# Sixteen 4x8 pixel groups per partition in place of eight 8x8 ones, with the Newton steps on VectorE, in a fused four-layer kernel

## The reference

```python
x = x + L0(x, dx, angle)      # every pixel of the image, rotated and shifted, bilinear:
    # out = g(iy0,ix0)*(wy0*wx0) + g(iy0,ix1)*(wy0*wx1) + g(iy1,ix0)*(wy1*wx0) + g(iy1,ix1)*(wy1*wx1)
    # with g(y, x) the pixel, or 0 outside of the image
x = x + L1(x, expert)         # relu(x wi^T + common and expert LoRA) wo^T + common and expert LoRA
x = x + L2(x, kind)           # softmax(mask(tanh(x W1 + b1) v)) x / count
x = x + L3(x, language)       # h = x + relu(x w1 + b1) w2 + b2;
    # (h - mean) * rsqrt(var + 1e-5) * gamma + beta, over the 512 columns
```

## Time and profile before

| | |
|---|---|
| median of 3 runs | 2329.93 us (2317.05 to 2334.8) |
| profiled execution | 2330.62 us, span 2328.9 us, granted TensorE clock 0.948 |
| share of the span | PE 92%, DVE 84%, POOL 41%, ACT 38% |
| chain that ended last | PE 40%, DVE 38%, issue 13%, DVE's sequencer 5% |
| DMA | 303.63 MB, mean 130 GB/s |

### The profile page before, as it was taken

How to read it: one execution, slowest core, us unless ns; L and a number is a source line. 1 busy time by engine, 2 the same in 40 slices (tenths; PEclk the granted TensorE clock), 3 DMA queues, 4 the chain that set the end, 5 groups by cost and what they waited for, 6 DMA issues and landing times.

```text
span 2328.9 us, 53794 instructions
## 1 busy us (share of the span) xinstructions
PE 2142.4 (92%) x15230; PEld 1350.8 (58%) x15230; DVE 1964.8 (84%) x6594; ACT 874.8 (38%) x2292; POOL 948.5 (41%) x1066
## 2 busy tenths in 40 slices
PE   7679999989989999999999899899999999999996
PEld 2345666656555665665556566565665655566663
DVE  7578899889889898889988898898988888899943
ACT  1323444434333443343334334343433333344431
POOL 3424454354354345435342443444445443444201
PEclk6559999999999999999999999999999999999997
DMA  8673555565455556545555655565566445554322
GB/s 223 154 203 94 127 138 138 127 149 126 122 124 134 124 132 151 126 118 128 142 128 118 151 126 135 111 138 133 133 136 147 123 110 132 129 132 116 101 72 63
DMA packets 336494, 303.63 MB, mean 130 GB/s; under 512 B 187295, under 2 KB 255977, under 8 KB 335767
## 3 DMA queue, kind: packets, MB, share of 16 engines
q1 hardware_dynamic: 290358, 184.05, 32.6%
q0 software_dynamic: 42624, 109.35, 20.1%
q10 hardware_dynamic: 3168, 6.29, 0.9%
HBM read 273.73 MB, written 65.70 MB: 146 GB/s over the span
## 4 chain that ended last, share of the span: by engine, by line
PE 40%; DVE 38%; issue 13%; DVEq 5%; SPq 2%; DMA 1%; another core or an unknown queue 0%; ACT 0%; POOL 0%; POOLq 0%; ACTq 0%
DVE work L853 14%; PE bank L1343 13%; PE bank L1380 13%; DVE work L866 3%; DVE work L867 3%; DVE work L865 3%; PE bank L1374 2%; PE bank L1199 2%; DVEq L849 2%; PE bank L1301 2%; DVEq L838 2%; DVE work L809 2%; DVE warp_sum L880 1%; PE bank L1275 1%; DVE hidden_parts L913 1%
## 5 line engine op out<-in xcount | busy, mean ns | idle before, releaser
L1343 PE MATMUL bank<-x1T,wiT 128*128 128x256 f16 x6144 | 764.5, 275 | 18.0 <-issue 17.2
L1380 PE MATMUL bank<-woT,hidden_parts 128*128 128x512 f16 x3072 | 759.8, 384 | 0.0
L853 DVE TENSOR_TENSOR work<-work 128x72 f32<-128x72 f32 x4096 | 683.2, 282 | 72.6 <-issue 50.6
L584 POOL DMA_INDIRECT work<-strips,gather_now x512 | 676.9, 1322 | 158.9 <-issue 136.3
L1343 PEld LDWEIGHTS bank<-x1T,wiT 128*128 128x128 f16 x6144 | 601.5, 99 | 165.9 <-issue 70.9
L1167 ACT ACTIVATE hidden<-bank 128x256 f32<-128x256 f32 x512 | 196.1, 383 | 774.7 <-PE bank L1350 446.3
L1380 PEld LDWEIGHTS bank<-woT,hidden_parts 128*128 128x128 f16 x3072 | 260.2, 98 | 301.8 <-issue 11.4
L580 POOL TENSOR_TENSOR gather_now<-group_now,no_offset 128x8 int32<-128x8 int32 x64 | 30.5, 476 | 801.3 <-DVE work L853 801.3
L913 DVE TENSOR_TENSOR hidden_parts<-hidden,hidden_parts 128x512 f16<-128x512 f32 x256 | 176.7, 690 | 29.4 <-ACT hidden_parts L1169 13.7
L1169 ACT ACTIVATE hidden_parts<-bank 128x256 f16<-128x256 f32 x512 | 195.1, 381 | 0.0
L1374 PE MATMUL bank<-hidden_parts,experts 128*32 128x128 f16 x2048 | 151.0, 226 | 0.0
(11 more groups left out here) (191 smaller groups left out, 2394.0 us busy)
## 6 DMA issues: line engine op xcount, KB each, us to landing
strips<-in_x_dram SPq DMA_DIRECT2D x64, 532.0 KB
lw<-in_L_cond_W_dram SPq DMA_DIRECT2D x128, 256.0 KB, 3.1
xs<-in_x_dram SPq DMA_DIRECT2D x64, 256.0 KB
experts<-ib_dram SPq DMA_DIRECT2D x64, 256.0 KB
gamma_b<-in_L_cond_gamma_dram SPq DMA_DIRECT2D x64, 256.0 KB, 4.4
x<-in_L_cond_beta_dram POOLq DMA_DIRECT2D x64, 256.0 KB, 5.7
out_dram<-y SPq DMA_DIRECT2D x64, 256.0 KB, 2.5
work<-strips,gather_now POOLq DMA_INDIRECT x512
```

The costliest lines, as they stand in the source:

```text
L584: g.indirect_dma_start(out=win[:, k, gi, :], out_offset=None, in_=flat, in_offset=bass.IndirectOffsetOnAxis(at, 0)).then_inc(gathered[k], 16)
L853: last = v.tensor_tensor(prods[:, :, :, j, :, row].rearrange("p a b g -> p g b a"), seen, wx.unsqueeze(2).broadcast_to([128, NG, TAPS, TAP ...
L1343: t.matmul(b[:, 0:2 * T], wiT[:, ws, m, tile(f)], x1T[:, xs_, m, :], start=(m == 0 and ws + xs_ == 0), stop=False)
L1380: last = t.matmul(down_ps[k][:, :], hidden_parts[:, hs, f % RING, k * T:(k + 1) * T], woT[:, ws, f, :], start=(first and n == 0), stop=False)
```

## The change

- A partition's pixels are 16 groups of 4x8 (`GC` columns, `GR` rows). An image has 32 offsets in place of 64, and a product covers 144 values in place of 72. There are 16 windows of 128 x 226 values per image in place of 8 of 128 x 348, each by its own indirect DMA. Strips are 64 wide, three DMAs per image. The tables of groups double.
- The three Newton steps go from POOL to DVE (three small operations each). The guess, the steps and `finish(i-2)` stand behind `add_pooled(1)`.
- DVE's loop takes four pairs per turn, 6 turns in place of 13.
- The setup's temporaries lie in `work`, 1024 wide in place of 512.

```diff
-GP = 8
-NG = 8
-Q = GP * GP
+GC, GR = 4, 8
+NG = 16
+Q = GC * GR
...
-SW, SS = 76, 32
+SW, SS = 64, 32
...
-RUN = 4 * SW + 44
+RUN = 3 * SW + 34
...
-                src = bass.AP(img.tensor, img.offset, [[SS, NS - 5], [D, T], [1, SW]])
-                sp.dma_start(strips[s, 2:NS - 3, rows, :], src).then_inc(strips_in[s], 16)
+                src = bass.AP(img.tensor, img.offset, [[SS, NS - 3], [D, T], [1, SW]])
+                sp.dma_start(strips[s, 1:NS - 2, rows, :], src).then_inc(strips_in[s], 16)
...
-            def deviations(c):
...
             def body(i, q):
                 if there(i, 2):
                     add_beta(i - 2, q)
-                    deviations(i - 2)
...
-                        products(0, 0, 0, 16)
+                        products(0, 0, 0, 8)
...
-                    if there(i, 2):
-                        guess_deviations()
...
                     if tail:
                         mask_scores(0)
-                    if there(i, 2):
-                        finish(i - 2)
                     if tail:
                         mask_scores(1)
...
                 if tail:
                     add_pooled(1)
+                if there(i, 2):
+                    deviations()
+                    finish(i - 2)
                 if warp:
                     products(1, 0, 0, HALF // 2)
...
+                def deviations():
...
+                    for step in range(3):
+                        link(v.tensor_tensor(newton[:, :], rstd[:, :], rstd[:, :], ALU.mult))
+                        link(v.scalar_tensor_tensor(newton[:, :], newton[:, :], -0.5, var_eps[:, :], ALU.mult, ALU.mult))
+                        link(v.scalar_tensor_tensor(rstd[:, :], newton[:, :], 1.5, rstd[:, :], ALU.add, ALU.mult))
...
-            with dve.Fori(2, NP // 2 - 1) as i:
-                body(i * 2 - 1, 1, first=False)
-                body(i * 2, 0)
-                body(i * 2 + 1, 1, second=False)
+            with dve.Fori(1, NP // 4 - 1) as i:
+                body(i * 4 - 1, 1, first=False)
+                for n in range(3):
+                    body(i * 4 + n, n % 2)
+                body(i * 4 + 3, 1, second=False)
```

More of the change, by code:

```diff
@@ L391, in load_strips @@
                 rows = slice(PADY, PADY + T)
-                src = bass.AP(img.tensor, img.offset, [[SS, NS - 5], [D, T], [1, SW]])
-                sp.dma_start(strips[s, 2:NS - 3, rows, :], src).then_inc(strips_in[s], 16)
-                for n in range(2):
-                    before = LEFT - n * SS
-                    sp.dma_start(strips[s, n, rows, before:SW], img[:, 0:SW - before]).then_inc(strips_in[s], 16)
-                    left = LEFT - n * SS
-                    sp.dma_start(strips[s, NS - 3 + n, rows, 0:left], img[:, D - left:D]).then_inc(strips_in[s], 16)
+                src = bass.AP(img.tensor, img.offset, [[SS, NS - 3], [D, T], [1, SW]])
+                sp.dma_start(strips[s, 1:NS - 2, rows, :], src).then_inc(strips_in[s], 16)
+                sp.dma_start(strips[s, 0, rows, LEFT:SW], img[:, 0:SW - LEFT]).then_inc(strips_in[s], 16)
+                sp.dma_start(strips[s, NS - 2, rows, 0:SS], img[:, D - SS:D]).then_inc(strips_in[s], 16)
             def load_pix(a, k, par):
@@ L564, in _ @@
             for k in range(2):
[L565 removed]
+                pool.wait_ge(strips_in[k], 48)
             for t in range(KT):
@@ L720, in floor @@
                 link(v.tensor_tensor(whole, whole, over, ALU.subtract))
-            xs_flat = xs[:, 1, :, :].rearrange("p k d -> p (k d)")
-            x1T_flat = x1T[:, :, :, :].rearrange("p s k t -> p (s k t)").bitcast(fp32)
             M = B * NG
             shape = lambda t: t.rearrange("p (b g) -> p b g", g=NG)
-            pos, other = xs_flat[:, 0:M], xs_flat[:, M:2 * M]
-            whole, whole_i = x1T_flat[:, 0:M], x1T_flat[:, M:2 * M].bitcast(i32)
-            at_f = y[:, 1, 0:M]
+            pos, other, whole, whole_i, at_f = (work[:, (n + 4) * M:(n + 5) * M] for n in range(5))
+            whole_i = whole_i.bitcast(i32)
             for ax in range(2):
@@ L794, in _ @@
             evacuate_low(11)
-            regs = [ctx.enter_context(v.register(f"window_offset{n}")) for n in range(LOADED)]
-            tap = taps.rearrange("p (x t j g i) -> p x t j g i", x=2, t=TAPS, g=NG, i=GP)
+            regs = [ctx.enter_context(v.register(f"window_offset{n}")) for n in range(HALF)]
+            tap = taps.rearrange("p (x t j g i) -> p x t j g i", x=2, t=TAPS, g=NG, i=GR)
             tap_rows = taps.rearrange("p (x t m) -> p x t m", x=2, t=TAPS)
-            prods = prod.rearrange("p (a b j g i) -> p a b j g i", a=TAPS, b=TAPS, g=NG, i=GP)
+            prods = prod.rearrange("p (a b j g i) -> p a b j g i", a=TAPS, b=TAPS, g=NG, i=GR)
             by_column_tap = prod.rearrange("p (a b m) -> p a b m", a=TAPS, b=TAPS)
@@ L845, in products @@
                     for m in range(start, end):
-                        j, row = m // GP, m % GP
+                        j, row = m // GR, m % GR
                         if m == 0:
@@ L981, in body @@
                             load_offsets(0, part)
-                        products(0, 0, 0, 16)
+                        products(0, 0, 0, 8)
                     if warp:
-                        products(0, 0, 16, 24)
+                        products(0, 0, 8, 12)
                     if ffn:
@@ L991, in body @@
                             residual(k)
-                    if there(i, 2):
-                        guess_deviations()
                     if warp:
-                        products(0, 0, 24, HALF)
+                        products(0, 0, 12, HALF)
                     hidden_low(0)
@@ L1008, in body @@
                 if warp:
-                    products(0, 1, 0, 8)
+                    products(0, 1, 0, 4)
                 hidden_low(2)
                 if warp:
-                    products(0, 1, 8, HALF)
+                    products(0, 1, 4, HALF)
                     take_offsets(1)
@@ L1029, in body @@
                 if warp:
-                    products(1, 1, 0, 24)
+                    products(1, 1, 0, 12)
                 hidden_low(6)
                 if warp:
-                    products(1, 1, 24, HALF)
+                    products(1, 1, 12, HALF)
                 if tail:
@@ L1050, in body @@
                 if ahead:
-                    products(0, 0, 0, 16, w + 1)
+                    products(0, 0, 0, 8, w + 1)
                 if ffn:
@@ L1057, in _ @@
             body(3, 1, second=False)
-            with dve.Fori(2, NP // 2 - 1) as i:
-                body(i * 2 - 1, 1, first=False)
-                body(i * 2, 0)
-                body(i * 2 + 1, 1, second=False)
-            body(NP - 3, 1, first=False)
-            for i in range(NP - 2, NP + 2):
+            with dve.Fori(1, NP // 4 - 1) as i:
[3 more added lines that the diff above has]
+                body(i * 4 + 3, 1, second=False)
+            body(NP - 5, 1, first=False)
+            for i in range(NP - 4, NP + 2):
                 body(i, i % 2)
```

71 lines of the change are left out of this document (25 added, 46 removed).

## The result

The changed kernel takes 2934.52 us (median of 4 runs, 2914.08 to 2949.42) against 2323.91 us of the kernel before on the same chip: a ratio of 1.262, interval 1.256 to 1.267. The forecast was 2326, with a range to 2390. It is 609 us off in the time, and none of the four cases in it is what happened. The times in this document are medians of all runs; one of four runs of `paced` (2851 us) was in a slower state of the chip, and its ratio leaves it out.

The account below looks back on a forecast made before the run. PE and DVE run level, DVE slightly ahead as the bound. From 2330.6 us, some 30 pairs give -16.5, setup +15 and the end -3, so 2326 us; range 2250 to 2390.

Parts of the forecast that it names:

- four cases: Forecast of 2326 us (0.46), no adapter wait (0.25), clock brought down (0.23), POOL late with its gathers (0.06).
- Gathers: On POOL, 16 gathers per image take 20 to 30 us in place of 10 to 16; cost nothing, covered by slack.
- The new wait at the adapter product: PE waits for adapter loads queued on SP behind the moved finish: 2.7 us per pair, 2.1 before an allowance for gathers.
- the sign that I named: PE's adapter product waiting 2 to 3 us for the adapter's transfers in nearly all of 29 pairs.
- S: Start of PE's second pooled product; `y` ready at S + 5.7, first adapter at S + 13.2, PE there at S + 11.1.
- Products: On DVE, 144 values at 0.23 us each, bounds 0.22 and 0.314; DVE gains 5.4 us per pair, bounds 6.0 and 0.
- VectorE's turn: Loop turn every fourth pair, not second: two PE waits of 3.97 us at the pooled product go per four pairs (-7.9).
- Newton on VectorE: Nine more small operations cost DVE 1.8 us per pair; guess and finish only moved; DVE's net gain 3.6 us.
- Setup: Larger group tables and 8 more first gathers before the loop: net +15 us, between +8 and +24; first L1391 at 176.
- The sum: Four pairs 268.1 us, 0.55 less per pair, a pair at 67.0; with setup and end, 2326 us.
- C, the clock: Rival: adapter waits near 4 us bring PE's granted clock to 0.95; 2400 us or somewhat under; chance 0.23.
- D, POOL late: Rival: 16 gathers of image 0 take 36 us, so the next pair's first products wait; 2370 and more; chance 0.06.

Follow-up runs that it names:

- paced: The changed kernel with a pause of 24 small memsets on POOL between an image's eighth and ninth gather; 2818 us, ratio 1.206 to the kernel before.
- late_pace1: The changed kernel with one small memset on POOL ahead of each gather but an image's first; 2349 us, ratio 1.004 to the kernel before.
- split_windows: The kernel before with each window fetched in two halves, so 16 gathers per image and the same bytes; 2661 us, ratio 1.140.
- no_groups: The kernel before with everything of the change but the groups, so still 8 gathers per image; 2447 us, ratio 1.050.
- no_groups_early: The kernel before with Newton steps on VectorE and four pairs per turn, but guess, steps and finish at their old places; 2322 us, ratio 0.997.
- loop4_only: The kernel before with only VectorE's loop changed, four pairs per turn in place of two; 2315 us, ratio 0.987.

## Why the prediction was wrong, step by step

**Gathers: "Cost nothing; the slack is the cover".** This is the step that failed: the term that I put at nothing was worth 585 us, the distance from the changed kernel to `late_pace1`. I priced the 512 further gathers as POOL's and the DMA engines' time only. As such they were what I had: undisturbed 0.95 + 0.30 us each, POOL at 41%, DMA half busy, and no wait for gathered windows in the middle of the run. What they cost lies on the engines that don't gather. From about the tenth of a row PE and SP, and in part VectorE, go on in steps of 0.70 us, for some 10 us, twice in most pairs. Two things seem to make it worse than twice the number: 16 follow each other without a break, which `paced` bears out, and VectorE has fewer runs of products left to hold them up (mean of a gather 1047 ns, 1322 before), for which `split_windows` speaks (1356 ns, 82 steps). I had read the gathers of 5.02 us as POOL's loss; by this they kept the rate down. A sign of it stood in the trace before, in "issue" at the transposes and L1343, which I put down to the loop's turn.

The rule of the Trainium skill, page "SBUF — State Buffer", section "Who interferes with whom", on the port that VectorE and GpSimd share, names those two engines alone. Here PE and SP are slowed, also while VectorE is busy for only 3.32 of 16 us (the fourth window above), so what I had weighed by that rule doesn't bear on the loss.

**The new wait at the adapter product.** Right in size, once the gathers are spaced: in `late_pace1` PE waits 64.3 us there in 25 waits that the profile puts down to the transfer, 2.6 each, where 2.7 were forecast (7 more are called "issue", one of them 8.2 us long). In the changed kernel itself the sign that I named is absent: its adapter product L1291 waits for the transfer once, for 0.7 us. In `no_groups` one pair reads so, PE's timeline first, then VectorE's and PE's again:

```profile
1316.54 1.10 PE L1282 MATMUL bank<-x,probsT 128*128 128x512 f32 x2
```

```profile
1322.00 1.41 DVE L942 SCALAR_TENSOR_TENSOR y<-y,rstd,x 128x512 f32<-128x512 f32 x2
```

```profile
1330.17 1.16 PE L1299 MATMUL bank<-xT,lw 128*128 128x128 f32 x8 [2.46 <-DMA gamma_b<-in_L_cond_gamma_dram]
```

From S = 1316.54, `y` is ready at S + 6.9 and the adapter product starts at S + 13.6; I had 5.7 and 13.2. But the place costs more than that wait where the rest is tight: 125 us in `no_groups` against `no_groups_early`. The expert inputs, queued on SP behind the same loads, are late there too, and my sum had no term for them:

```profile
PE bank L1372 <- DMA experts<-ib_dram: 22.8, 10, 4.6
PE bank L1372 <- issue: 16.2, 12, 2.5
```

**Products.** Mis-sized. 4 of them take 1.22 us and 12 take 3.33 in the changed kernel:

```profile
1308.99 1.22 DVE L823 TENSOR_TENSOR work<-work 128x144 f32<-128x144 f32 x4
1310.65 3.33 DVE L823 TENSOR_TENSOR work<-work 128x144 f32<-128x144 f32 x12
```

That is (3.33 - 1.22) / 8 = 0.264 us from one to the next, between my 0.23 and the bound of 0.314. Per pair 16.9 us in place of 20.1: 3.2 won, not 5.4. In the earlier trace rows 72 values take 0.157 us; each further value costs 1.49 ns, more than the 1.04 of the line that I drew to the plain adds. VectorE's busy time per pair confirms it: over the 23 middle pairs of `late_pace1` it is 58.1 us (1335.46 in all), of the kernel before 59.4 (1365.77). That is 1.3 less, and 3.2 - 1.8 gives 1.4; I had forecast 3.6 less, and under 56. The rule that I had weighed (Trainium skill, "VectorE: DVE Perf Modes", "The TRN2 errata") puts it at an estimated 210 ns, and the trace does not agree: the measured price is 264.

**VectorE's turn.** Too dear. I took away two waits of 3.97 us in four pairs, the one whole wait that I had read, but the earlier trace rows has 33.0 us in 17 waits, 1.9 each. `loop4_only` has 17.6 us in 15 waits in that row and gains 1.3% in all, some 25 us, just at the lower end of the 25 to 40 that I had for it. **Newton on VectorE**: `no_groups_early` is 1.0% above `loop4_only` by the ratios, some 23 us, or 0.7 per pair; the nine operations are 1.8 us of VectorE's time.

**Setup.** The first L1364 starts at 177.65, 16.5 us later than before (161.11); I had 176. With the gathers spaced it is 169.18 in `late_pace1`.

**The sum.** Leave the harm of the gathers' rate out, as I did, and the number stands: `late_pace1` has 67.6 us per pair ((1941.4 - 387.1) / 23 by the row below) against my 67.0, and 2349 us against 2326, inside the forecast's range. That agreement is in part luck, since one memset per gather also takes away the 44 us that the kernel before was losing, and the smaller gains from the products and the turn work the other way. A pair then takes what it took before (67.57), so nothing is left of the 0.55 us that I had won.

```profile
L943 DVE TENSOR_SCALAR var_eps<-mv x24: 157/213/382, 387.1 to 1941.4; 128x2 f32<-128x2 f32 x24
```

**The rivals.** C, the clock, had the granted clock fall with each long wait, and it does (0.869 over the run, 0.948 before), but as a follower of the steps. D, POOL late, didn't happen: POOL is idle for 1114.2 us waiting for windows. I had bounded the gathers by what POOL and the transfers need, and had not asked what a row of them does to the other engines.

**Left open.** What it is that 16 gathers in a row take from the other sequencers, and why their instructions then come 0.70 us apart, no run here shows. It starts between spacings of 1.25 and 1.58 us; the exact rate wasn't sought. Rows of 8 at 1.25 us do little harm (8 steps in the kernel before, 44 in 62 such rows of `paced`). Whether it is a backlog that drains, and how fast, stays open; a kernel whose every row of 8 ends in a pause, between the images too, wasn't run.

## What to carry to other kernels

When a change multiplies instructions on an engine with much idle time, ask what they do to the others, and measure it by the cheapest means: put a small operation between them and see. "Issue" before plain instructions on several engines at once is a symptom to look at even where it adds up to 2% only (44.8 us in two rows of the kernel before); here spacing the gathers was worth 2.9%, with the longer loop, to the kernel that had been there all along. And an operation that is moved has two queues to satisfy: here the adapter's loads wait behind `finish` on SP, while `finish` itself waits for beta behind the gathers on POOL, so that neither place is free.

## What the runs showed of the hardware

- Indirect DMAs that POOL starts every 1.25 us slow PE and SP to one instruction per 0.70 us after 7 to 15 of them in a row in the changed kernel (340 such steps on PE). At 1.58 us they don't (3 steps), and rows of 8 do it little (8 steps in the kernel before). Half the bytes (2965 us) or half the rows (3036 us) of a gather make it no better than the 2935 us of the changed kernel, and plain small DMAs from POOL in between do no harm (2297 us).
- The DMA engines need not be busy for that: their share was 0.51 and 0.55 in the slow stretches.
- A product of 144 values with small inner pieces comes at 0.264 us, one of 72 at 0.157: 1.7 times, for twice the values.
